# Rows of odd steps by a repeating transfer instead of a TensorE spread

## The reference

```
xr, gate = split(x @ W_in.T);  xr = xr + t_emb
xc = silu(causal depthwise convolution of xr, 4 taps, + b_conv)
xn = layernorm(xc) * ln_g + ln_b                       # 8 x 1024 x 1024
Bm, Cm, dt = split(xn @ W_xproj.T)                     # 16 states each
Ad = 1 + tanh(dt @ W_dt.T + b_dt) * 0.01 * -tanh(A_log)
Bd = Bm * min(norm(xn), 1)
for each token: h = clip(h * Ad + Bd (outer) xn, -10, 10);  y = Cm . h
out = (y + D * xn) * silu(gate) @ W_out.T
```

## Time and profile before

| | |
|---|---|
| median of 3 runs | 6185.2 us (6185.17 to 6187.26) |
| the profiled execution, its own time | 6190.74 us |
| its span, first to last instruction | 6188.9 us |
| first update to last clamp | 3323 to 6099 us |
| busy in the whole span | PE 94%, PEld 44%, DVE 72%, ACT 39%, POOL 52% |
| granted TensorE clock, mean | 0.972 |

### The profile page before, as it was taken

One profiled execution on the slowest core, in us unless ns is written; L12 is line 12 of the kernel. 1 busy time (PEld: TensorE's weight loads), 2 busy tenths in 40 slices (PEclk: granted clock), 3 DMA queues, 4 the chain that ended last, 5 costly groups with the idle time before them and its releaser, 6 DMA issues. The chain is left out here.

```text
span 6188.9 us, 73250 instructions
## 1 busy us (share of the span) xinstructions
PE 5830.7 (94%) x24000; PEld 2703.2 (44%) x24000; DVE 4474.3 (72%) x5676; ACT 2407.5 (39%) x4698; POOL 3217.6 (52%) x2625
## 2 busy tenths in 40 slices
PE   7999999999999999999986879999999999999998
PEld 3444444444444444444443424444443444444343
DVE  4656656556556566565546998999999898999983
ACT  2444444445444454444453424243332423334111
POOL 1876767677667776775743323425243443524213
PEclk7999999999999999999988889999999999999999
DMA  2332323333232332323213343534444443544433
GB/s 86 89 91 69 99 73 94 91 88 89 76 96 77 98 93 69 106 60 96 82 67 109 87 113 103 147 96 131 110 116 126 121 133 89 150 96 128 115 91 115
DMA packets 411565, 613.30 MB, mean 99 GB/s; under 512 B 58768, under 2 KB 189968, under 8 KB 410672
## 3 DMA queue, kind: packets, MB, share of 16 engines
q1 hardware_dynamic: 374320, 558.24, 32.4%
q10 hardware_dynamic: 36864, 50.38, 3.2%
HBM read 305.31 MB, written 201.38 MB: 82 GB/s over the span
## 5 line engine op out<-in xcount | busy, mean ns | idle before, releaser
L1126 POOL TENSOR_TENSOR acc<-acc,prob 128x512 f32<-128x512 f32 x1536 | 1906.4, 1277 | 837.3 <-PE bank L815 570.8
L1055 DVE TENSOR_REDUCE mx<-bank 128x1 f32<-128x512 f32 x2048 | 1307.4, 684 | 535.9 <-PE bank L785 529.6
L2091 DVE SCALAR_TENSOR_TENSOR g<-xps,bd,g 128x1024 f32<-128x1024 f32 x1024 | 1313.2, 1282 | 143.8 <-PE xps L1806 68.1
L1806 PE MATMUL xps<-sx,spread 128*128 128x512 f32 x2048 | 910.4, 529 | 140.6 <-DVE g L2091 126.0
L948 ACT ACTIVATE prob<-misc 128x512 f32<-128x512 f32 x1277 | 713.5, 599 | 739.0 <-PE misc L802 653.6
L785 PE MATMUL bank<-khat,qhat 96*128 96x512 f32 x2048 | 939.1, 519 | 5.9 <-DVE mx L1055 0.9
L2097 DVE TENSOR_SCALAR g<-g,lim 128x1024 f32<-128x1024 f32 x1024 | 892.7, 872 | 34.8
L1806 PEld LDWEIGHTS xps<-sx,spread 128*128 128x128 f32 x2048 | 359.0, 195 | 693.8 <-issue 368.0
L802 PE MATMUL misc<-qhat,khat 98*128 98x512 f32 x1443 | 602.6, 460 | 17.8 <-ACT prob L948 11.7
L785 PEld LDWEIGHTS bank<-khat,qhat 96*128 96x128 f32 x2048 | 373.8, 192 | 532.5 <-issue 381.4
L1820 PE MATMUL yps<-g,cexp 128*32 128x512 f32 x4096 | 585.4, 630 | 0.1
(11 more groups left out here) (221 smaller groups left out, 7189.6 us busy)
## 6 DMA issues: line engine op xcount, KB each, us to landing
sx<-scratch_xhl SPq DMA_DIRECT2D x512, 128.0 KB, 4.9
scratch_dx<-dx SPq DMA_DIRECT2D x64, 512.0 KB, 3.2
scratch_xhl<-xhi SPq DMA_DIRECT2D x64, 512.0 KB, 4.9
scratch_xhl<-xn SPq DMA_DIRECT2D x64, 512.0 KB, 5.1
scratch_y<-ysb SPq DMA_DIRECT2D x512, 64.0 KB
dx_t<-scratch_dx SPq DMA_DIRECT2D x59, 512.0 KB, 6.1
y_t<-scratch_y SPq DMA_DIRECT2D x59, 512.0 KB, 3.9
xt_n<-in_x SPq DMA_DIRECT2D x112, 256.0 KB, 3.0
```

Source lines behind the costliest of these rows:

```text
L1055: dve.tensor_reduce(self.mx2[:, h * TT + qt, c:c + 1], bank[m][:, 0:QC], AX.X, ALU.max).then_inc(sem[f"dve_m{m}"], 1)
L1126: pool.tensor_tensor(self.acc[:, a, h, :], self.acc[:, a, h, :], self.prob[:, (n % 2) * GH + h, :], ALU.add).then_inc(sem["pool_acc"], 1)
L1806: mm = pe.matmul(self.xps[t % 2][:, half * BANK:(half + 1) * BANK], self.spread[:, 2 * part + half, :], self.sx[:, n % 2, wd, :], start=Tr ...
L2091: dve.scalar_tensor_tensor(self.g[:, t % 4, :], self.xps[t % 2][:, :], self.bd[:, i % 2, tl:tl + 1], self.g[:, (t - 1) % 4, :], ALU.mult, ...
```

## The change

- Only even tokens go by hi, lo, `sx` and `xps`. The stores `shi` and `slo` write every second partition, `sx` holds half as many tokens, and `xps` buffers alternate over even tokens, so that row t + 4 can be made once update t is done.
- Odd tokens: a new piece `sxr` stores the odd rows of `xn` as float32 to `scratch_xrow` after `a2`; `lo`, which overwrites `xn`, now waits for that store to land. A new piece `lr` for each odd step loads the row of all 8 batches and repeats each 16 times (512 KB in SBUF) into one of four buffers `xb`, once the update eight steps before is done. The update of an odd step reads `xb` from SBUF.
- The waits ahead of an update stand in another order: the clamp of the step before first, then the row.
- To make room, `y_t` and `dx_t` share memory with setup tensors, and all constants come on one semaphore for which every engine waits in full.

```diff
+                    put("SP", 0.55, ("sxr", i, hb, bb), (("a2", i, hb, bb, 1),) + ((("sxr", i, hb, bb - 2),) if bb > 1 else was("sxr", *old, HB - 2 + bb)), [(f"st_xr{bb % 2}", 16)], lands=4.0)
...
-                        put("POOL", 1.27, ("lo", i, hb, bb, half), (("hi", i, hb, bb), ("sq", i, hb, bb), ("a3", i, hb, bb, half)),
+                        put("POOL", 1.27, ("lo", i, hb, bb, half), (("hi", i, hb, bb), ("sq", i, hb, bb), ("a3", i, hb, bb, half), ("sxr", i, hb, bb)),
...
+        def row(t):
+            i = t // TOK
+            put(t - 7.0, "SP", 0.6, ("lr", t), tuple(("sxr", i, hb, bb) for hb in range(2) for bb in range(HB)) + (
+                (("q", t - 2 * ROWS),) if t > 2 * ROWS else ()), [(f"ld_xb{t // 2 % ROWS}", 16)], lands=4.0)
...
-            put(t - 2.0, "PE", 0.45, ("x", t), (("lu", t // UNIT),) + ((("q", t - 2),) if t > 1 else ()), [("pe_xps", 1)])
+            put(t - 2.0, "PE", 0.45, ("x", t), (("lu", t // UNIT),) + ((("q", t - 4),) if t > 3 else ()), [("pe_xps", 1)])
...
-            put(t, "DVE", 1.3, ("q", t), (("x", t),) + ((("g", t - 1),) if t else (("g0",),)) + ((("d3", i),) if tl == 0 else ()) + (
+            put(t, "DVE", 1.3, ("q", t), (("lr", t) if t % 2 else ("x", t),) + ((("g", t - 1),) if t else (("g0",),)) + ((("d3", i),) if tl == 0 else ()) + (
...
-        self.sx = sb("sx", [P, 2, UNIT // 2, BANK], F32R)
+        self.sx = sb("sx", [P, 2, UNIT // 4, BANK], F32R)
+        self.xb = sb("xb", [P, ROWS, DIN])
...
+                sp.dma_start(d["xrow"][hb * HB + bb, i * TOK // 2:(i + 1) * TOK // 2, :], self.xn[1:P:2, bb, :]).then_inc(
+                    sem[f"st_xr{bb % 2}"], 16)
...
+                sp.dma_start(self.xb[:, k, :], d["xrow"][:, t // 2, :].unsqueeze(1).broadcast_to([B, NST, DIN])).then_inc(
+                    sem[f"ld_xb{k}"], 16)
...
-                w.wait_ge(sem["dve_set"], plan.after("dve_set", ("g0",)))
-                w.wait_ge(sem["pe_xps"], plan.after("pe_xps", ("x", t)))
-                w.wait_ge(sem["dve_par"], plan.after("dve_par", ("d3", i)))
                 if t:
                     w.wait_ge(sem["dve_g"], plan.after("dve_g", ("g", t - 1)))
+                if t % 2:
+                    k = t // 2 % ROWS
+                    row = self.xb[:, k, :]
+                    w.wait_ge(sem[f"ld_xb{k}"], plan.after(f"ld_xb{k}", ("lr", t)))
+                else:
+                    row = self.xps[t // 2 % 2][:, :]
+                    w.wait_ge(sem["pe_xps"], plan.after("pe_xps", ("x", t)))
+                w.wait_ge(sem["dve_set"], plan.after("dve_set", ("g0",)))
+                w.wait_ge(sem["dve_par"], plan.after("dve_par", ("d3", i)))
                 if t > 3:
                     w.wait_ge(sem["pe_y"], plan.after("pe_y", ("out", (t - 4) // 2 * 2)))
-                dve.scalar_tensor_tensor(self.g[:, t % 4, :], self.xps[t % 2][:, :], self.bd[:, i % 2, tl:tl + 1],
+                dve.scalar_tensor_tensor(self.g[:, t % 4, :], row, self.bd[:, i % 2, tl:tl + 1],
                                          self.g[:, (t - 1) % 4, :], ALU.mult, ALU.add).then_inc(sem["dve_q"], 1)
...
-        w.wait_ge(sem["ld_const"], 48)
-        w.wait_ge(sem["ld_cols"], 48)
+        w.wait_ge(sem["ld_const"], 176)
```

More of the change, by code:

```diff
@@ L1378, in load @@
             put(n * UNIT - 12.0, "SP", 2.2, ("lu", n), (rows if n * UNIT % TOK == 0 else ()) + (
-                (("x", (n - 1) * UNIT - 1),) if n > 1 else (("rest",),)), [(f"ld_sx{n % 2}", 64)], lands=4.0)
+                (("x", (n - 1) * UNIT - 2),) if n > 1 else (("rest",),)), [(f"ld_sx{n % 2}", 64)], lands=4.0)
+        def row(t):
+            i = t // TOK
+            put(t - 7.0, "SP", 0.6, ("lr", t), tuple(("sxr", i, hb, bb) for hb in range(2) for bb in range(HB)) + (
+                (("q", t - 2 * ROWS),) if t > 2 * ROWS else ()), [(f"ld_xb{t // 2 % ROWS}", 16)], lands=4.0)
         def x_of(t):
-            put(t - 2.0, "PE", 0.45, ("x", t), (("lu", t // UNIT),) + ((("q", t - 2),) if t > 1 else ()), [("pe_xps", 1)])
+            put(t - 2.0, "PE", 0.45, ("x", t), (("lu", t // UNIT),) + ((("q", t - 4),) if t > 3 else ()), [("pe_xps", 1)])
         for n in range(2):
             load(n)
-        x_of(0), x_of(1)
+        for t in range(1, 2 * ROWS, 2):
+            row(t)
+        x_of(0), x_of(2)
         for t in range(last):
             i, tl = divmod(t, TOK)
-            put(t, "DVE", 1.3, ("q", t), (("x", t),) + ((("g", t - 1),) if t else (("g0",),)) + ((("d3", i),) if tl == 0 else ()) + (
+            put(t, "DVE", 1.3, ("q", t), (("lr", t) if t % 2 else ("x", t),) + ((("g", t - 1),) if t else (("g0",),)) + ((("d3", i),) if tl == 0 else ()) + (
                 (("out", (t - 4) // 2 * 2),) if t > 3 else ()), [("dve_q", 1)], step=t)
-            if t + 2 < last:
-                x_of(t + 2)
+            if t % 2 and t + 2 * ROWS < last:
+                row(t + 2 * ROWS)
+            if t % 2 == 0 and t + 4 < last:
+                x_of(t + 4)
             put(t, "DVE", 0.82, ("g", t), (("q", t),), [("dve_g", 1)], port=True)
@@ L1459, in __init__ @@
         self.mask = sb("mask", [P, 8, 32])
[L1460 to L1462 removed]
+        self.ones_at = early[:, DIN:DIN + 4 * P]
+        self.tmp = early[:, DIN + 4 * P:DIN + 4 * P + CT * NX].rearrange("p (t k) -> p t k", t=CT)
+        self.ones = early[:, DIN + 4 * P + CT * NX:DIN + 5 * P + CT * NX]
         self.gw = sb("gw", [P, NX])
@@ L1523, in __init__ @@
         self.sem = self.plan.sems
-        for name in ("win", "const", "late", "wx", "cols", "sc", "spread", "wxdt"):
+        for name in ("win", "const", "late"):
             name = f"ld_{name}"
@@ L1605, in sync @@
                 w.wait_ge(sem["pool_lo"], plan.after("pool_lo", ("lo", i, hb, bb, 1)))
-                sp.dma_start(d["xhl"][1, hb * HB + bb, i * TOK:(i + 1) * TOK, :].bitcast(F32), self.xn[:, bb, :]).then_inc(
-                    sem[f"st_xlo{bb}"], 16)
+                sp.dma_start(d["xhl"][1, hb * HB + bb, i * TOK // 2:(i + 1) * TOK // 2, :].bitcast(F32),
+                             self.xn[0:P:2, bb, :]).then_inc(sem[f"st_xlo{bb}"], 16)
+            elif kind == "sxr":
+                i, hb, bb = at
+                w.wait_ge(sem["pool_x"], plan.after("pool_x", ("a2", i, hb, bb, 1)))
+                w.wait_ge(sem.get(f"st_xr{bb % 2}"), plan.before(f"st_xr{bb % 2}", p))
+                sp.dma_start(d["xrow"][hb * HB + bb, i * TOK // 2:(i + 1) * TOK // 2, :], self.xn[1:P:2, bb, :]).then_inc(
+                    sem[f"st_xr{bb % 2}"], 16)
+            elif kind == "lr":
+                t, = at
+                i, k = t // TOK, t // 2 % ROWS
+                for hb in range(2):
+                    for bb in range(HB):
+                        w.wait_ge(sem[f"st_xr{bb % 2}"], plan.after(f"st_xr{bb % 2}", ("sxr", i, hb, bb)))
+                if t > 2 * ROWS:
+                    w.wait_ge(sem["dve_q"], plan.after("dve_q", ("q", t - 2 * ROWS)))
+                sp.dma_start(self.xb[:, k, :], d["xrow"][:, t // 2, :].unsqueeze(1).broadcast_to([B, NST, DIN])).then_inc(
+                    sem[f"ld_xb{k}"], 16)
             elif kind == "lu":
                 n, = at
-                i, s, t0, wd = n * UNIT // TOK, n % 2, n * UNIT, UNIT // 2
+                i, s, t0, wd = n * UNIT // TOK, n % 2, n * UNIT // 2, UNIT // 4
                 for hb in range(2):
@@ L1616, in sync @@
                 if n > 1:
-                    w.wait_ge(sem["pe_xps"], plan.after("pe_xps", ("x", (n - 1) * UNIT - 1)))
+                    w.wait_ge(sem["pe_xps"], plan.after("pe_xps", ("x", (n - 1) * UNIT - 2)))
                 else:
@@ L1798, in tensor @@
                 n, r = divmod(t, UNIT)
-                part, wd = divmod(r, UNIT // 2)
+                part, wd = divmod(r // 2, UNIT // 4)
+                if t > 3:
+                    w.wait_ge(sem["dve_q"], plan.after("dve_q", ("q", t - 4)))
                 w.wait_ge(sem["dve_set"], plan.after("dve_set", ("rest",)))
                 w.wait_ge(sem[f"ld_sx{n % 2}"], plan.after(f"ld_sx{n % 2}", ("lu", n)))
-                if t > 1:
-                    w.wait_ge(sem["dve_q"], plan.after("dve_q", ("q", t - 2)))
                 for half in range(2):
-                    mm = pe.matmul(self.xps[t % 2][:, half * BANK:(half + 1) * BANK], self.spread[:, 2 * part + half, :],
+                    mm = pe.matmul(self.xps[t // 2 % 2][:, half * BANK:(half + 1) * BANK], self.spread[:, 2 * part + half, :],
                                    self.sx[:, n % 2, wd, :], start=True, stop=True)
```

38 lines of the change are left out of this document (19 added, 19 removed).

## The result

The changed kernel takes 6476.65 us (median of 4 runs, 6474.3 to 6479.77) against 6186.23 us for the kernel before on the same chip: ratio 1.0469, 95% interval 1.0452 to 1.0485. It is 290 us slower; 248 us were forecast. The profiled execution's span is 6477.9 us. The recurrence runs from 3325.4 to 6390.0 us, 3065 us instead of 2776: all of the loss lies there. Behind the total, though, stand two costs of which the prediction named one.

A forecast was written before the change was run, and what follows sets the result against it. It took the recurrence to be bound by a chain on VectorE (update, clamp, side work). Terms 293 + 4 - 65 + 8 + 8 = +248 us gave 6439 us profiled, 6433 us as median; range 6300 to 6560.

The forecast's parts named there:

- collision term: Recurrence, odd updates reading SBUF beside GpSimd: 302 long operations at 0.92 us and 57 short at 0.26, +293 us.
- odd share: GpSimd operations of the recurrence beside odd updates: half, 336 and 63, less a tenth, so 302 long and 57 short.
- the term's upper end: Highest loss per long GpSimd operation beside an odd update, 0.99 us, when GpSimd goes first.
- The update itself: Odd updates with two SBUF tensors, undisturbed: 8 ns more, 512 times, +4 us (bounds -13 to +20).
- half-rate rival: Odd updates with two SBUF tensors run at half rate: 553 us more, 6986 us; chance 0.03.
- TensorE's relief: TensorE without the spread of odd steps: VectorE's waits for spread rows and projections shrink, -65 us (bounds 0 and -112).
- wait order: Waits ahead of each update, clamp's first: another wait behind costs 0 to 0.05 us, 0 to 51 us; +8 taken.
- The transfers: Added 512 KB row loads of odd steps in the recurrence: mostly hidden, 0 us taken.
- rival for late rows: Odd-step row loads: every fourth row 1 us late would add 128 us, 6561 us; chance 0.07.
- estimate of 72% load: Transfer engines in the recurrence: 42.4% plus 36% for the rows, less 6% saved, gives 72%, below full.
- The rows before the first step: GpSimd's chain before the recurrence: lo waits for the odd-row store, 5 to 17 us more, +8 taken.
- The constants: Start of the kernel: all engines wait for all eleven small loads, hidden by the end of attention, 0 us.

The follow-up runs named there:

- e2: The changed kernel with the update's waits in the order of the kernel before (clamp last): 6522.0 us, ratio 1.0539.
- e6: The changed kernel, even rows spread a step later, odd updates reading the previous even step's PSUM row (wrong row), row loads a sixteenth: 6093.1 us, ratio 0.9832.
- e1: The kernel before with the update's wait for the last clamp put first: 6176.8 us, ratio 0.9977.
- corner runs: The changed kernel with odd rows read from SBUF or PSUM, at full or a sixteenth traffic: SBUF 6477 and 6323 us, PSUM 6429 and 6093 us.
- e9: The changed kernel, even rows spread a step later, odd updates reading PSUM rows (wrong row), row loads carrying half the channels: 6116.1 us, ratio 0.9878.
- e4: The changed kernel, even rows spread a step later, odd updates reading the previous even step's PSUM row (wrong row), full traffic: 6429.4 us, ratio 1.0392.
- e12: The changed kernel with only every fourth step's row by repeating transfer, two xb buffers, other rows by TensorE: 6462.0 us, ratio 1.0430.

## Why the prediction was right, and where it was not

**The collision term (293 us): the right mechanism, a quarter too large.** VectorE's busy time rose by 262 us, 209 of it on the odd steps that the term counts, and removing the collisions where nothing hides them gave 230. A clamp behind a GpSimd operation lost 0.83 us (1.64 against 0.81), not 0.89 to 0.99. The odd share was as taken: 298 of the 672 long and 56 of the 126 short operations beside odd updates, against 302 and 57. The Trainium skill, "SBUF — State Buffer", section "Who interferes with whom", adds that the order of issue decides who blocks; the traces agree, if a start within some 45 ns counts for GpSimd: when e2 makes the update 55 to 68 ns later, GpSimd goes first in 154 odd updates instead of 51, 103 of them with its record 40 or 41 ns behind the update's, and the loss moves from clamps to updates. VectorE's groups in e2:

```profile
L2129 DVE TENSOR_SCALAR g<-g,lim 128x1024 f32<-128x1024 f32 x1022 | 1012.2, 990 | 34.8
L2123 DVE SCALAR_TENSOR_TENSOR g<-xb,bd,g 128x1024 f32<-128x1024 f32 x511 | 791.0, 1548 | 41.7 <-DMA xb<-scratch_xrow 1.1 <-DVE g L2129 0.9
```

Here the prediction had luck. It took VectorE to go first because GpSimd starts some 40 ns behind the update; by e2, a start 40 ns behind means that GpSimd goes first, and the loss is 1.10 us, over the term's upper end of 0.99. It was the new order of the waits that put the update ahead, so that GpSimd starts 108 ns or more behind it in most odd steps. With the old order the odd steps cost 242 us more than in the kernel before instead of 209.

**The update itself (+4 us):** 0 in fact; the median of odd and even updates is 1283 ns. The half-rate rival is refuted.

**TensorE's relief (-65 us): about right where nothing hides it.** Spread waits did nearly vanish, and e6 shows 100 us for relief and wait order together; with 15 to 45 us for the wait order, 55 to 85 are left for the relief. What came with it was not as forecast: TensorE was busy 88% of a stretch (351.94 of 400 us) and not some 75%, at a granted clock of 0.94 instead of 0.99, on which the text put no price. A chunk took 389 to 394 us in the middle of the recurrence, where 386 were expected.

**The wait order (+8 us): wrong sign.** The text took each wait behind the clamp's as an added cost. What counts is which wait the instruction itself carries: with the clamp's carried, the gap is 36 ns, otherwise 91 or 104. That is worth 15 us before (e1) and 45 us in the changed kernel (e2 against 6477); the latter is not the gap alone, since e2's odd steps are also 33 us longer by its costlier collisions.

**The transfers (0 us): the step that failed, though the total held.** "Mostly hidden; I take 0", with a rival for late rows. The rows were never late (1.4 us in all), and the estimate of 72% load was even above the 59.8% found. But it asked only whether the new transfers arrive in time, not what they do to the old ones. The loads of side work had been placed with 3 to 5 us to land and lost that; TensorE's queue stood behind them. Alone this costs 336 us, more than the collisions. That the total still came out within 44 us is so because the two hide each other (153 us for the traffic once the collisions are there) and because relief and wait order gave 100 instead of 57: 230 + 153 - 100 = 283, beside the 290 measured. (These three come from the same corner runs, so the sum shows how the parts lie, and is no check of them.) A total within 44 us is thus partly luck: the forecast had 293 for collisions and 0 for traffic, the runs 230 and 153.

**The rows before the first step (+8 us):** GpSimd waits 6.00 us once for the row store and ends 7.7 us later, but the first update comes 1.9 us later, at 3325.4: from the last `lo` to it there are 10.0 us instead of 15.7. I put that down to the halved `sx` loads; no run tests it.

**The constants (0 us):** as said.

## What to carry to other kernels

Moving an operand from PSUM to SBUF can turn an instruction into one that excludes GpSimd: look at what GpSimd does beside it, and take the price from an instruction of the same kind that already collides. A transfer that is itself early can still cost, through the old ones that it delays: compare their landing times with what the order of work allows, and don't expect the cost to go with the bytes (23 us for half, 336 for all). When two limits lie close, undo both and each one alone; a single undo (48 of 230 us here) tells little of a cause's size.

## What was not expected of the hardware

- The wait that an instruction carries itself is cheap, one in a separate instruction before it is not: 36 ns against 91 to 104 ns from clamp to update, by the order of two waits in the code.
- Which of two instructions goes first is not simply which record starts first: in the changed kernel and e2, GpSimd goes first in all 123 odd steps where its first operation's record starts 27 to 44 ns after the update's, and in none where it starts 48 ns or more after it.
- Landing times turn sharply: with 34, 51 and 61.5% of the engines' time in use (e6, e9, e4) the same 256 KB load lands in 3.1, 3.4 and 7.8 us. The share alone doesn't set it: in e12 it is 6.3 us at 64.6%.
- A late load can cost TensorE its clock as well: behind 10.23 us of idle time the granted clock was 0.54 for 4.1 us.
- Bytes are a poor measure of that load: 381 MB took 64.6% of the engines' time in e12, 374 MB took 51.0% in e9.
